# Maximum and first exponential of the 896-column tile ahead of the last clamps and of the weighing; seed ahead of both; gathered transposes evacuated on VectorE; end reordered

## The reference

```python
x = L0_attn_qkv
xn = _layernorm(x, axis=-1)
s = _L0_attn_ref(xn, ...)          # 16 heads of 16, ALiBi, causal
g = _silu(_L0_ffn_ref(xn, ...))    # 32 experts, top 4, capacity 128, and a shared one of 704
x = x + s * g
```

```python
attn = jnp.maximum(jax.nn.softmax(scores, axis=-1), 1e-10)
attended = jnp.einsum('bhqk,bhkd->bhqd', attn, v)
return attended @ out_w.T + out_b
```

```python
g = jnp.einsum('ech,ehf->ecf', buf, w_gate)
u = jnp.einsum('ech,ehf->ecf', buf, w_up)
y = jnp.einsum('ecf,efh->ech', jax.nn.silu(g) * u, w_down)
out = jnp.zeros((T, Hq), x.dtype).at[tok].add(gath * wv[:, None])
```

## Time and profile before

| | us |
|---|---|
| median of 3 runs (644.6 to 648.15) | 646.54 |
| the profiled execution | 642.44 |
| its span in the trace | 640.8 |

### The profile page before, as it was taken

The page is one execution under the profiler, slowest core; times in us unless marked ns, Lnnn a source line. Parts: engine busy times, 40 slices in busy tenths (PEclk is TensorE's granted clock), DMA queues, the critical chain, the costliest instruction groups (busy, mean ns, idle before and its releaser), DMA issues.

```text
span 640.8 us, 17285 instructions
## 1 busy us (share of the span) xinstructions
PE 562.8 (88%) x4584; PEld 384.2 (60%) x4584; DVE 475.2 (74%) x1066; ACT 452.6 (71%) x1053; POOL 269.1 (42%) x632
## 2 busy tenths in 40 slices
PE   1699559688999899999999999999999999999992
PEld 1694227555666566666666666666666666666661
DVE  5997964657777867886787788777867886787465
ACT  2322564358877878887888788878888887888670
POOL 7630000215445355445544554455455345544403
PEclk9759869789999999999999999999999999999997
DMA  8991256552335334433444343434433436731147
GB/s 258 167 253 59 99 155 195 132 135 60 88 90 111 91 86 87 105 90 89 102 100 97 91 103 84 92 83 102 98 90 87 105 91 199 192 77 23 26 137 135
DMA packets 79537, 71.47 MB, mean 112 GB/s; under 512 B 18114, under 2 KB 70020, under 8 KB 79492
## 3 DMA queue, kind: packets, MB, share of 16 engines
q1 hardware_dynamic: 70292, 59.30, 34.1%
q0 software_dynamic: 9136, 11.80, 12.1%
q10 hardware_dynamic: 80, 0.03, 0.0%
HBM read 47.82 MB, written 23.59 MB: 111 GB/s over the span
## 4 chain that ended last, share of the span: by engine, by line
PE 49%; ACT 20%; issue 12%; DVE 10%; DMA 4%; SPq 3%; ACTq 1%; DVEq 0%; POOLq 0%; POOL 0%
ACT PSB L1062 10%; PE PSB L897 7%; PE PSB L791 6%; ACT PB L1071 6%; PE PSB L765 5%; PE PSB L813 5%; PE PSB L868 4%; PE PSB L810 4%; PE PSB L787 3%; PE PSB L889 3%; PE PSB L850 2%; PE PSB L666 2%; PE PSB L761 2%; DVE WDS L1281 2%; SPq L497 1%
## 5 line engine op out<-in xcount | busy, mean ns | idle before, releaser
L1346 DVE TENSOR_REDUCE NEGM<-PSB 128x1 f32<-128x1024 f32 (+7 forms) x256 | 192.2, 751 | 58.6 <-PE PSB L765 57.6
L1062 ACT ACTIVATE PSB<-PSB,NEGM 128x1024 f32<-128x1024 f32 (+7 forms) x256 | 183.5, 717 | 35.6 <-DVE NEGM L1346 35.4
L1071 ACT ACTIVATE PB<-PSB 128x128 f32<-128x128 f32 (+7 forms) x256 | 166.8, 653 | 35.5 <-PE PSB L791 33.6
L1352 DVE TENSOR_SCALAR PB<-PB 128x128 f32<-128x128 f32 (+7 forms) x256 | 114.2, 455 | 45.9 <-ACT PB L1071 44.4
L765 PE MATMUL PSB<-STACKS 111*128 111x512 bf16 (+3 forms) x384 | 105.8, 330 | 0.0
L791 PE MATMUL PSB<-STACKS 111*128 111x512 bf16 (+3 forms) x384 | 104.2, 326 | 0.0
L787 PE MATMUL PSB<-MK,IDB 128*128 128x128 bf16 x256 | 57.5, 225 | 22.7 <-ACT PSB L1062 16.4
L1656 POOL DMA_INDIRECT moe_rows<-YE,IDX x32 | 56.9, 1777 | 29.3 <-issue 29.3
L810 PE MATMUL PSB<-PB,VH 128*32 128x256 f32 x640 | 67.8, 384 | 0.0
L787 PEld LDWEIGHTS PSB<-MK,IDB 128*128 128x128 bf16 x256 | 24.5, 96 | 63.7 <-ACT PB L1071 39.2
L761 PE MATMUL PSB<-MQ,IDB 128*128 128x128 bf16 x256 | 58.2, 227 | 0.9 <-ACT UL L1049 0.5
(11 more groups left out here) (200 smaller groups left out, 1171.6 us busy)
## 6 DMA issues: line engine op xcount, KB each, us to landing
STACKS<-q_parts SPq DMA_DIRECT2D x192, 32.0 KB, 1.9
STACKS<-k_parts SPq DMA_DIRECT2D x192, 32.0 KB, 1.8
WGU<-in_L_ffn_w_gate_dram SPq DMA_DIRECT2D x32, 176.0 KB
WGU<-in_L_ffn_w_up_dram SPq DMA_DIRECT2D x32, 176.0 KB
WDS<-in_L_ffn_w_down_dram SPq DMA_DIRECT2D x32, 176.0 KB
q_parts<-PB SPq DMA_DIRECT2D x8, 384.0 KB, 2.6
XN<-in_L_attn_qkv_dram SPq DMA_DIRECT2D x4, 512.0 KB, 5.7
moe_rows<-XN SPq DMA_DIRECT2D x1, 2048.0 KB, 8.8
```

Of the source, the lines that this page charges most:

```text
L1062: act.activation(sc, sc, ACT.Exp, bias=NEGM[:, par, i:i + 1], accum_out=LSUM[:, par, i:i + 1]).then_inc(exp1_done, 1)
L1071: act.activation(PB[:, k % 2, prob_offset(s):prob_offset(s) + (s + 1) * P], psf[:, base:base + (s + 1) * P], ACT.Exp).then_inc(exp2_done, 1)
L1346: dve.tensor_reduce(NEGM[:, par, i:i + 1], psf[:, base:base + (i + 1) * P], AX_X, ALU.max, negate=True).then_inc(max_ready, 1)
L1352: dve.tensor_scalar(p, p, FLOOR, 0.0, ALU.subtract, ALU.max).then_inc(clamp_done, 1)
```

## The change

On ACT, `weigh` moves from its place between exp2 and exp1 at s = 1 to behind exp1 of 896 columns, and exp_seed so comes first. The copy of the transposes leaves ACT (s = 2, ahead of exp2). On DVE the copy comes in at s = 2, behind the maximum of 768 columns, as `turn_rows`; at s = 1 the maximum of 896 columns comes first, and the clamp of 1024 columns of the unit before, which stood at the end of s = 0, follows it. At the end the four early products of batch 0 come ahead of gates 4 to 7, the first two of them ahead of the last heads. PE, POOL and SP have the same lists as before.

```diff
@@ scalar, phase @@
-                    if s == 2 and exists(it, w):
-                        o = aux_task(it, w, TR)
-                        act.activation(XET[:, :, :].rearrange("p c m -> p (c m)"), o[:, 0:D], ACT.Copy)\
-                            .then_inc(xet_ready, 1)
...
-                    if s == 1 and exists(it, w - 1):
-                        weigh(it, w - 1)
                     if s == 1 and exists(it, k + 1) and not (isinstance(it, int) and k == UNITS - 2):
                         exp_seed(it, k + 1)
                     if exists(it, k + 2):
                         exp1(it, k + 2, s)
+                    if s == 1 and exists(it, w - 1):
+                        weigh(it, w - 1)
@@ vector @@
+            def turn_rows(it, k):
+
+                b, before = aux(it, k, TR)
+                dve.wait_ge(aux_ready[b], before + 1)
+                dve.tensor_copy(XET[:, :, :].rearrange("p c m -> p (c m)"), PSB[:, AUX + b, 0:D]).then_inc(xet_ready, 1)
@@ vector, phase @@
                     if isinstance(it, int) and k == UNITS and s == 1:
-                        for g in (4, 5):
-                            gate(g)
+                        for g in range(2):
+                            early_product(g)
+                    late = exists(it, k + 2) and exists(it, k - 1)
+                    if s == 1 and late:
+                        row_max(it, k + 2, s)
+                        clamp(it, k - 1, NQ - 1)
                     if s > 0 and exists(it, k):
                         clamp(it, k, s - 1)
-                    if exists(it, k + 2):
+                    if exists(it, k + 2) and not (s == 1 and late):
                         row_max(it, k + 2, s)
                     if s == 0 and exists(it, w - 1):
                         shared(it, w - 1, SB)
-                    if s == 0 and exists(it, k - 1):
+                    if s == 0 and exists(it, k - 1) and not late:
                         clamp(it, k - 1, NQ - 1)
+                    if s == 2 and exists(it, w):
+                        turn_rows(it, w)
@@ vector, after the phases @@
-            for g in range(6, NT // 2):
+            for g in range(2, NT // 4):
+                early_product(g)
+            for g in range(NT // 4, NT // 2):
                 gate(g)
-            for g in range(NT // 4):
-                early_product(g)
```

## The result

| | before | after |
|---|---|---|
| median of the runs side by side, us | 645.57 (643.0 to 648.15) | 656.89 (655.18 to 657.76) |
| ratio, with its 95% interval | | 1.0172 (1.0124 to 1.0220) |
| span of the profiled execution, us | 640.8 | 653.5 |
| DVE busy, us | 475.2 | 488.5 |
| ACT busy, us | 452.6 | 451.0 |

What follows compares the result with a forecast made beforehand. PE's list bounds the loop (busy 95%), with short stops for ACT. Terms +2.7 ordinary, +2.3 down, +2.0 phases -1 and 0, -1.5 end sum to +5.5 us; on the 646.54 median, 652.0, range 642.5 to 659.

Steps and rivals of the forecast that it cites:

- the late weighing: Rival, chance 0.13: on ACT the weighing starts late behind exp1, adding 0.23 us a phase; sum +12.2, 658.7 us.
- Ordinary phases, +0.13 each: In 21 ordinary loop phases SA waits for YE, so pass 2 s = 4 starts 0.13 us later; +2.7 us.
- the stall: On PE, SA waits for YE, ready 0.83 us later behind exp1 of 896; SA starts 0.29 us later.
- Down phases, +0.29 each: In 8 down phases SA starts 0.29 us later and all of it goes through; +2.3 us.
- The seed comes 1 us earlier, and POOL's chain with it, but PE turns its result only behind the first half of GU; zero.: On ACT and POOL in the loop: earlier seed and chain change nothing, zero us, as PE turns the result later.
- No transfer is moved in the loop: In the loop: sequences of PE, SP and POOL unchanged and no transfer moved; no cost counted.
- Phases -1 and 0, +2.0: Before the loop: weighing behind an exp1 awaiting its maximum; each phase costs 0.13 to 1.66 us, 1.0 taken, +2.0.
- The end, -1.5: After the loop: early products and POOL's transfers start earlier; head's stores delayed 0.5, costing 0.3; -1.5 us, between +1 and -2.7.
- The edits priced at zero on DVE: In DVE's loop: later clamps zero, at worst 0.1 us a phase; transposes' copy zero, uncovered up to 0.42.
- the stall is paid in down phases only: Rival, chance 0.27: in the loop the 0.13 us of ordinary phases is lost; sum +1.8, 648.3 us.
- The ACT stretch decides: Rival, chance 0.15: PE absorbs the wait on SA, pass 2 s = 4 comes 0.3 us earlier; -6.8, 639.7 us.

Runs made afterwards that it cites:

- Experiment 9: Changed kernel with POOL's gather held until DVE's maximum of 256 columns is done: 648.04 us, ratio 1.0101 to the kernel before.
- experiment 8: Changed kernel with the weighing in its old place, ahead of exp1, in phases -2 to 0 only: 651.7 us, ratio 1.0143 to the kernel before.
- experiments 6: Changed kernel with ACT order seed, weighing, exp1, and the copy of the transposes back on ACT: 646.73 us, ratio 1.0051 to the kernel before.
- experiment 7: Changed kernel with ACT order seed, weighing, exp1, and the maximum of 896 columns back behind the clamps: 642.02 us, ratio 0.9997 to the kernel before.
- experiments 5: Kernel before with one edit, the seed ahead of the weighing and exp1 of 896 columns: 643.56 us, ratio 1.0008.
- experiment 10: Gather held until the maximum of 256 columns: kernel before with seed first, 638.69 us, ratio 0.9946; changed kernel with seed, weighing, exp1 order, 637.65 us, ratio 0.9928.
- experiment 3: Changed kernel with the weighing put back ahead of exp1 of 896 columns, behind the seed: 632.85 us, ratio 0.9858 to the kernel before.

## Why the prediction was right in sign and short in size

The range and the side were right, the time was 5 us short. That the time lies inside the range is in part luck: the range reached up to 659 for the sake of the late weighing, which didn't happen, and the delay of the stores, 10 us that the sum had at zero, fitted into that room. In the order of the sum:

- **Ordinary phases, +0.13 each.** Right within the reading. Experiment 9 has the stall without the collision: 14.77, 14.72, 14.63 against 14.59, 14.77, 14.53 of before, in the mean +0.08; in 21 phases 1.6 us for 2.7. The kernel before has part of the late landing itself: pass 2 starts 3.38 to 3.49 us behind the first store in its phases second behind a down one, and 3.28 where it waits for nothing. Without that I estimate the stall at 0.18, 0.09 and 0.12, so that it is paid in ordinary phases too. It was right, too, that the earlier exp1 is stopped by SA. The net hides a gain and a loss: versions with the seed first and no stall take 14.39, 14.40 and 14.32, so that the stall costs 0.34 a phase against what the seed alone would have reached.
- **Down phases, +0.29 each.** Right: 16.45 in experiment 9 against 16.15, +0.30, 2.4 us in all.
- **"The seed comes 1 us earlier, and POOL's chain with it, but PE turns its result only behind the first half of GU; zero."** This is the step that failed. I followed the chain to its first reader, and not to what stands behind it in POOL's list: scatter, two copies and the gather. "No transfer is moved in the loop" was true of the lists and false of the times. The gather moved by 1.2 to 1.6 us against the stores and onto them. After minus experiment 9, the three kinds of phases that see it are 0.49, 0.52 and 0.42 longer, the one behind the down phase 0.01; with seven of each in the loop that is 10 us, the largest term of all.
- **Phases -1 and 0, +2.0.** Mis-sized: 28.8 us for 25.3, +3.5, of which the weighing has 2.7 (experiment 8). The phases absorbed less than I had assumed. Phase -1 shows the mechanism as forecast: SA's first load waits 1.87 us for YE, where it waited 0.19 before:

```profile
137.80 0.47 ACT L1113 ACTIVATE YE<-PSB,XES 128x256 f32<-128x256 f32 x1
```

```profile
138.32 0.29 PEld L889 LDWEIGHTS PSB<-XFH,SWGH 128*128 128x128 f32 x1 [1.87 <-ACT YE L1113]
```

- **The end, -1.5.** Right in sum (-1.4 alone), wrong in both parts. I gave the head's stores a delay of 0.5 and a cost of 0.3; they lost 1.9, and the first product came 3.0 us late. The last stores gained 3.5 in the median. The Trainium skill ("DMA: Bandwidth & Descriptors", Issuing engines are not separate DMA queues) says that transfers interleave on the same 16 engines whichever engine starts them, and the trace agrees in both directions: 16 KB in 4.0 us for 2.1 beside POOL's transfers, 256 KB in 2.1 for 5.6 without them.
- **The edits priced at zero on DVE** (order of clamps and maximum, the copy) are worth zero in the steady phases by themselves (experiments 6 and 7, behind a down phase). In the others their versions differ by 0.3 to 0.8 us a phase, with the offset of the gather.

The terms make +1.6 + 2.4 + 10 + 3.5 - 1.5 = 16 us; the spans differ by 12.7. Of the rest, 1.3 is one phase of 17.46 us in the loop of before (others of its kind 16.15), 1.6 that phase -2 took 16.8 us there and 15.2 here, and 0.4 is left. Phase -2 took between 14.5 and 18.3 us in the 14 traces, and phases 4 and 5 had one such step in most of them; why, is open. It is why single traces are compared here by phases.

The rivals: *the stall is paid in down phases only* is answered above, by the three kinds of ordinary phases in experiment 9, though each difference is small. *The ACT stretch decides* would have had to give phases under 14.5, and they are longer, with the loads busy in only 253 of 406 us. The rule of the Trainium skill ("Perfetto Trace Analysis", Identifying the Most-Contended Engine), by which a PE with idle loads has time to give, would have misled here, as PE's list in order was held by single late releasers. *The late weighing* came near in time (658.7) for the wrong reason: the weighing started 1.00 behind exp1. Its observation was sound in the old place: there the weighing began 0.27 after DN and the address was computed in that gap. With the seed ahead it begins 0.1 sooner and exp1 of 896 with it 0.2, which is the gain of 0.2 a phase that experiments 5 and 10 show.

**A better version.** The order seed, weighing, exp1 with the rest of the change (experiment 3) ran 1.4% faster than before, interval 0.9818 to 0.9898. It rests on an offset of the gather that no wait secures; with the wait (experiment 10) 0.7% are left, interval 0.9896 to 0.9960, 3.5 us of the difference being the one slow gather of phase 26.

## What to carry to other kernels

When an instruction moves, follow the engine that it releases to the end of that engine's list, and look above all for the DMA starts in it: a transfer that moves by a microsecond in time can delay its neighbours, though no list changes. A dependent operation moved behind a long one costs the whole length of that one at its reader, unless the reader's slack, read in the trace, is longer. Where several edits shift the timing of one shared thing, judge them in stretches in which that thing can't be late (here the phase behind a down phase), or pin it down with a wait, before anything is said about their worth.

## What the runs showed of the hardware

Three stores of 2 KB each, issued within 1.4 us, land 3.12 us after the first issue, and at 3.4 to 4.05 when an indirect gather of 128 rows starts 0 to 0.9 us behind the first; from 1.4 us on they land at 3.12 to 3.35 in the phases of the table. The same gather takes 3.1 us in the other phases (median of before) and 8.1 to 8.6 when the second of two large transfers starts within 1.1 us behind it. Small operations of POOL don't have one length: in the same phase (k = 16) the copy of 128x2 indices took 0.56 us in experiment 7 and 1.21 in experiment 3, whose edits differ in DVE's order alone, and the gather behind it started 0.4 and 1.6 us behind the first store. So a new order on DVE went together with another start of a transfer on POOL; the cause of these lengths was not tested.
